# A test-time learner between transformer layers: products that share their stationary operand are made as one

## The reference

```
def recon(W1, b1, W2, b2, z):                 # W1 32x128, W2 128x32
    return z + gelu(z @ W1.T + b1) @ W2.T + b2

for x in batches:                             # 512 x 128, layer-normed
    z, y = x @ t_k.T, x @ t_v.T
    grads = gradient of mean((recon(params, z) - y)**2) in params
    params = params - 1e-3 * grads
    out = recon(params, x @ t_q.T)            # with the new params
```

## Time and profile before

| | |
|---|---|
| median of three runs | 2206.51 us (2203.84 to 2206.94) |
| the profiled execution | 2217.11 us |
| its span, first to last instruction | 2215.4 us |
| TensorE busy (PE) | 1622.4 us, 73% |
| VectorE busy (DVE) | 1256.2 us, 57% |
| ScalarE busy (ACT) | 1080.1 us, 49% |
| GpSimd busy (POOL) | 821.4 us, 37% |
| the learner's eight batches | L1209 of batch 0 starts at 595.32 us, L1248 of batch 7 at 772.22 us |

### The profile page before, as it was taken

How to read it: one execution, slowest core, us unless ns; L and a number is a source line. 1 busy time by engine, 2 the same in 40 slices (tenths; PEclk the granted TensorE clock), 3 DMA queues, 4 the chain that set the end, 5 groups by cost and what they waited for, 6 DMA issues and landing times. The chain is left out here.

```text
span 2215.4 us, 26050 instructions
## 1 busy us (share of the span) xinstructions
PE 1622.4 (73%) x8550; PEld 855.5 (39%) x8550; DVE 1256.2 (57%) x2743; ACT 1080.1 (49%) x2160; POOL 821.4 (37%) x1482
## 2 busy tenths in 40 slices
PE   2799999954499850715530159359999999979998
PEld 1133333213377640504430137213333333357776
DVE  3688888857443230054468812277787777535443
ACT  1377777745333330246650013127777776645554
POOL 3455555325433235170051775543444331012121
PEclk8699999986655555856755559659999999979999
DMA  3211111100000012000003112311111111010000
GB/s 97 72 67 66 66 66 65 42 1 1 1 1 0 1 56 76 29 8 1 0 2 115 38 39 23 54 71 46 54 59 58 57 58 54 13 40 10 6 10 15
DMA packets 85099, 85.21 MB, mean 38 GB/s; under 512 B 36071, under 2 KB 67665, under 8 KB 84837
## 3 DMA queue, kind: packets, MB, share of 16 engines
q1 hardware_dynamic: 75044, 76.43, 10.4%
q0 software_dynamic: 7680, 6.06, 1.7%
q10 hardware_dynamic: 2240, 1.05, 0.2%
HBM read 59.78 MB, written 25.17 MB: 38 GB/s over the span
## 5 line engine op out<-in xcount | busy, mean ns | idle before, releaser
L921 DVE TENSOR_REDUCE arena<-psum 128x2 f32<-128x1024 f32 x512 | 602.0, 1217 | 130.5 <-PE psum L720 125.8
L836 ACT ACTIVATE arena<-psum 128x512 f32<-128x512 f32 x1024 | 554.0, 595 | 141.4 <-PE psum L733 132.4
L733 PE MATMUL psum<-arena 99*128 99x512 bf16 x1024 | 312.6, 387 | 16.5 <-DMA arena<-arena 11.9
L720 PE MATMUL psum<-arena 72*128 72x512 bf16 x1024 | 286.9, 396 | 42.5 <-POOL arena L622 20.3
L743 PE MATMUL psum<-arena 128*32 128x512 f32 x2048 | 274.5, 608 | 3.0 <-ACT arena L836 1.9
L733 PEld LDWEIGHTS psum<-arena 99*128 99x128 bf16 x1024 | 74.8, 98 | 294.3 <-ACT arena L836 223.2
L720 PEld LDWEIGHTS psum<-arena 72*128 72x128 bf16 x1024 | 96.5, 101 | 184.8 <-DVE arena L921 28.5
L2409 ACT ACTIVATE arena<-arena 128x128 f32<-128x128 f32 x252 | 102.5, 481 | 103.2 <-POOL arena L2397 103.2
L2392 POOL TENSOR_SCALAR arena<-arena 128x4 f32<-128x4 f32 x80 | 22.5, 281 | 309.3 <-DVE arena L2386 304.8
L631 POOL TENSOR_TENSOR arena<-arena 128x16 bf16<-128x16 f32 x64 | 13.9, 218 | 316.5 <-DVE arena L921 222.2
L344 ACT ACTIVATE arena<-arena 128x128 f32<-128x128 f32 x192 | 76.7, 481 | 96.4 <-POOL arena L260 71.0
(11 more groups left out here) (440 smaller groups left out, 2723.2 us busy)
## 6 DMA issues: line engine op xcount, KB each, us to landing
arena<-L_q_parts SPq DMA_DIRECT2D x192, 96.0 KB
arena<-L_k_parts SPq DMA_DIRECT2D x192, 96.0 KB
L_q_parts<-arena SPq DMA_DIRECT2D x16, 384.0 KB, 3.3
L_k_parts<-arena SPq DMA_DIRECT2D x16, 384.0 KB, 3.3
arena<-in_L_ffn_w SPq DMA_DIRECT2D x1, 2048.0 KB
ec_result<-arena SPq DMA_DIRECT2D x1, 2048.0 KB
arena<-in_L_ffn_fc2s SPq DMA_DIRECT2D x1, 2048.0 KB, 16.5
ec_normed<-arena SPq DMA_DIRECT2D x1, 2048.0 KB
```

The source lines that it names most:

```text
L720: last = nc.tensor.matmul(bank[:, 512 * h:512 * h + 512], columns(q9[0:QK_ROWS], i, m // 2, 128 * (2 * (m % 2) + h), 128), columns(k9[0:QK ...
L733: nc.tensor.matmul(acts.bank(name), columns(k9[0:ROWS], i, g, 128 * k, 128), columns(q9[0:ROWS], i, g, 0, 512), start=True, stop=True).the ...
L836: nc.scalar.activation(prob[:, k % 2, g, :], acts.bank(name), ACT.Exp, scale=scale).then_inc(act_taken, 1)
L921: nc.vector.tensor_reduce(neg_max[:, i % 2, 2 * m:2 * m + 2], maxes.bank(("max", i, m)).rearrange("p (h t) -> p h t", h=2), axis=AX.X, op= ...
```

## The change

`y_map` is placed behind `u_map` in memory, so that one product of 64 columns with the turned tokens makes both the hidden sums and the part of `dh` that comes from the tokens; `hidden` makes it, and the four L1221 go. The accumulating group stays open until `hidden_gradient` adds the part with `m_map`; only the first tile's product has the start flag of the bank. `d_a` and `h_one` are placed beside each other per tile (65 columns), so that one product with the plain tokens makes both `nh` and the first gradient; `gradients` replaces `first_gradient` and `token_products`. The sums of one tile stand side by side in PSUM now (`a_dh`), and `nh`, `g` and `hh` are neighbours in bank 4. Waits: `y_done` moves ahead of `hidden`, `hT_done` ahead of all of `hidden_gradient`, `gradients` waits for `hh_done` and `da_done`, and ScalarE's copy of `nh` waits for the first gradient's copy on VectorE (`g_done`).

```diff
--- before.py
+++ after.py
@@ -1117,8 +1117,9 @@
     w2 = c.take(HID + 1)
     w2T = c.take(128)
     b1, b1_col = c.take(HID), c.take(1)
-    maps = c.take(2 * HID)
-    y_map, m_map = c.take(HID), c.take(HID)
+    three = c.take(3 * HID)
+    maps, uy_map, y_map = three[:, 0:2 * HID], three[:, HID:3 * HID], three[:, 2 * HID:3 * HID]
+    m_map = c.take(HID)
     q_map, u_map = maps[:, 0:HID], maps[:, HID:2 * HID]
 
     w_in, diff_done, turned, w_ready = sem("w_in"), sem("diff_done"), sem("turned"), sem("w_ready")
@@ -1168,9 +1169,10 @@
             nc.scalar.activation(y_map, c.bank(4)[:, 2 * HID:3 * HID], ACT.Copy).then_inc(maps_ready, 1)
             nc.scalar.activation(m_map[0:HID + 1, :], c.bank(4)[0:HID + 1, 3 * HID:4 * HID], ACT.Copy).then_inc(maps_ready, 1)
 
-    a, slope, d_a = c.take(128), c.take(128), c.take(128)
+    a, slope = c.take(128), c.take(128)
     a_sq, a_off, a_safe, gel, th, low, inv, phi, high, dens = (c.take(128) for _ in range(10))
-    h_one = c.take(TPB * (HID + 1)).rearrange("p (k h) -> p k h", k=TPB)
+    h_da = c.take(TPB * (2 * HID + 1)).rearrange("p (k h) -> p k h", k=TPB)
+    h_one, d_a = h_da[:, :, 0:HID + 1], h_da[:, :, HID + 1:2 * HID + 1]
     hT, hqT = c.take(S), c.take(S)
     d_sum, g_sum = c.take(HID), c.take(HID)
     nh_sum, hh_sum = c.take(HID + 1), c.take(HID + 1)
@@ -1179,7 +1181,7 @@
 
     ones_set, turned2, copied2, turned3, copied3 = sem("ones_set"), sem("turned2"), sem("copied2"), sem("turned3"), sem("copied3")
     summed2, summed3 = sem("summed2"), sem("summed3")
-    a_made, aT_made, q_made, dh_made, hh_made, nh_made = (sem(n) for n in ("a_made", "aT_made", "q_made", "dh_made", "hh_made", "nh_made"))
+    a_made, aT_made, q_made, dh_made, hh_made = (sem(n) for n in ("a_made", "aT_made", "q_made", "dh_made", "hh_made"))
     g_made, kg_made, gb_made, w2_made, o_made, y_made = (sem(n) for n in ("g_made", "kg_made", "gb_made", "w2_made", "o_made", "y_made"))
     a_done, hT_done, h_done, slope_done, hq_done = (sem(n) for n in ("a_done", "hT_done", "h_done", "slope_done", "hq_done"))
     sq_done, th_done, safe_done, gel_done, low_done, pool_step, step = (
@@ -1189,9 +1191,10 @@
 
     p_aT, p_a, p_q, p_o, p_w = (c.bank(n) for n in range(5))
     turn_bank, bias_bank = c.bank(5), c.bank(7)
-    dh, g, kg = p_a[:, 128:256], p_a[:, 256:288], p_a[:, 384:448]
+    a_dh = p_a[:, 0:256].rearrange("p (k h) -> p k h", k=TPB)
+    kg = p_a[:, 384:448]
     gb, gb_col = bias_bank[:, 0:HID], bias_bank[0:HID, HID:HID + 1]
-    nh, hh, g_w2 = p_w[:, 0:33], p_w[0:33, 64:97], p_w[:, 128:161]
+    nh_g, nh, g, hh, g_w2 = p_w[:, 0:65], p_w[:, 0:33], p_w[:, 33:65], p_w[0:33, 65:98], p_w[:, 128:161]
     y_new, m_new, w2T_new = p_w[:, 192:224], p_w[0:33, 256:288], p_w[0:33, 384:512]
 
     ROUNDS = B + 11
@@ -1205,8 +1208,10 @@
             def hidden(b):
                 pe.wait_ge(copied2, b + 1)
                 pe.wait_ge(moved, b)
+                pe.wait_ge(y_done, 3 * b)
                 for k in range(TPB):
-                    last = nc.tensor.matmul(p_a[:, 32 * k:32 * k + 32], tile_T(b, k), u_map, start=True, stop=True)
+                    last = nc.tensor.matmul(a_dh[:, k, :], tile_T(b, k), uy_map, start=(k == 0), stop=True,
+                                            skip_group_check=True)
                 last.then_inc(a_made, 1)
                 nc.tensor.matmul(p_aT[0:HID, :], u_map, c.nT[:, b, 1:S + 1], start=True, stop=True).then_inc(aT_made, 1)
 
@@ -1215,14 +1220,11 @@
                 nc.tensor.matmul(p_q[0:HID, :], q_map, c.nT[:, b, 1:S + 1], start=True, stop=True).then_inc(q_made, 1)
 
             def hidden_gradient(b):
-                pe.wait_ge(y_done, 3 * b)
                 pe.wait_ge(a_done, b + 1)
+                pe.wait_ge(hT_done, b + 1)
                 for k in range(TPB):
-                    nc.tensor.matmul(dh[:, 32 * k:32 * k + 32], tile_T(b, k), y_map, start=True, stop=False)
-                    if k == 0:
-                        pe.wait_ge(hT_done, b + 1)
-                    last = nc.tensor.matmul(dh[:, 32 * k:32 * k + 32], hT[0:HID + 1, 128 * k:128 * k + 128], m_map[0:HID + 1, :],
-                                            start=False, stop=True)
+                    last = nc.tensor.matmul(a_dh[:, k, HID:2 * HID], hT[0:HID + 1, 128 * k:128 * k + 128], m_map[0:HID + 1, :],
+                                            start=False, stop=True, skip_group_check=True)
                 last.then_inc(dh_made, 1)
 
             def hidden_products(b):
@@ -1231,17 +1233,12 @@
                     last = nc.tensor.matmul(hh, h_one[:, k, :], h_one[:, k, :], start=(k == 0), stop=(k == TPB - 1))
                 last.then_inc(hh_made, 1)
 
-            def first_gradient(b):
+            def gradients(b):
+                pe.wait_ge(hh_done, b + 1)
                 pe.wait_ge(da_done, b + 1)
                 for k in range(TPB):
-                    last = nc.tensor.matmul(g, c.n[:, TPB * b + k, :], d_a[:, 32 * k:32 * k + 32], start=(k == 0), stop=(k == TPB - 1))
+                    last = nc.tensor.matmul(nh_g, c.n[:, TPB * b + k, :], h_da[:, k, :], start=(k == 0), stop=(k == TPB - 1))
                 last.then_inc(g_made, 1)
-
-            def token_products(b):
-                pe.wait_ge(hh_done, b + 1)
-                for k in range(TPB):
-                    last = nc.tensor.matmul(nh, c.n[:, TPB * b + k, :], h_one[:, k, :], start=(k == 0), stop=(k == TPB - 1))
-                last.then_inc(nh_made, 1)
 
             def first_step(b):
                 pe.wait_ge(g_done, b + 1)
@@ -1300,8 +1297,7 @@
                 if inside(b):
                     hidden_gradient(b)
                     hidden_products(b)
-                    first_gradient(b)
-                    token_products(b)
+                    gradients(b)
                     first_step(b)
                 if inside(b - 1):
                     output(b - 1)
@@ -1351,7 +1347,8 @@
             def products(b):
                 act.wait_ge(hh_made, b + 1)
                 nc.scalar.activation(hh_sum[0:HID + 1, :], hh, ACT.Copy).then_inc(hh_done, 1)
-                act.wait_ge(nh_made, b + 1)
+                act.wait_ge(g_made, b + 1)
+                act.wait_ge(g_done, b + 1)
                 nc.scalar.activation(nh_sum, nh, ACT.Copy).then_inc(nh_done, 1)
 
             def output(b):
@@ -1430,7 +1427,7 @@
                 dve.wait_ge(a_made, b + 1)
                 if b >= 1:
                     dve.wait_ge(b_moved, 2 * b)
-                tt(by_tile(a), by_tile(p_a[:, 0:128]), b1.unsqueeze(1).to_broadcast([128, TPB, HID]), ALU.add).then_inc(a_done, 1)
+                tt(by_tile(a), a_dh[:, :, 0:HID], b1.unsqueeze(1).to_broadcast([128, TPB, HID]), ALU.add).then_inc(a_done, 1)
 
             def slopes(b):
                 dve.wait_ge(safe_done, b + 1)
@@ -1447,9 +1444,9 @@
             def hidden_gradient(b):
                 dve.wait_ge(slope_done, b + 1)
                 dve.wait_ge(dh_made, b + 1)
-                tt(d_a, dh, slope, ALU.mult).then_inc(da_done, 1)
+                tt(d_a, a_dh[:, :, HID:2 * HID], by_tile(slope), ALU.mult).then_inc(da_done, 1)
                 dve.wait_ge(da_done, b + 1)
-                nc.vector.tensor_reduce(d_sum, d_a.rearrange("p (k h) -> p h k", k=TPB), axis=AX.X, op=ALU.add).then_inc(sum_done, 1)
+                nc.vector.tensor_reduce(d_sum, d_a.rearrange("p k h -> p h k"), axis=AX.X, op=ALU.add).then_inc(sum_done, 1)
 
             def keep_gradient(b):
                 dve.wait_ge(g_made, b + 1)
```

## The result

The changed kernel takes 2191.65 us (median of 4 runs, 2188.68 to 2192.58), beside 2206.73 for the kernel before on the same chip (4 runs). The ratio is 0.992, with a 95% interval of 0.9903 to 0.9936, so it is 14 to 21 us faster. The forecast was 2194.3, or 12.2 us faster, with a range of 2186 to 2202.

What follows compares the result with a forecast made beforehand. TensorE's program order looked like the bound, with the slope chain close behind. Leg B 8.1 plus leg A 6.15 minus new waits 2.1 gave 12.2 us: 2206.5 to 2194.3, forecast 2189 to 2199, 8-in-10 range 2186 to 2202.

Steps and rivals of the forecast that it cites:

- leg B: First gradient's start to `first_step`: eight products become four, the copy of g becomes exposed; 25.73 us falls by 8.1.
- the bound of 1.8: Leg B at high clock: VectorE's reduction and norm statistics before the copy hold `first_step` at about 1.8 us.
- Leg A: `hidden`'s start to the first gradient: y products move into `hidden`, 33-row products stay; 6.15 us saved over the batches.
- The slope chain: Leg A: L1209, bias, square, GpSimd, reciprocals, L1445, then L1450; holds batches 1 to 3 at 8.1 us.
- The new wait: `hidden` waits for the y_done copies on ScalarE: 0.70 us each in batches 1 to 3, 2.1 lost.
- leg C: From `first_step` to the next `hidden`, containing the turn L1283; claimed to keep its instructions and length.
- the cover: Batches 4 and 5: the GpSimd chain hides `hidden`'s 1.85 us later start; without it, 1.85 lost in each.
- rival 2: The y_done wait passes through in batches 4 and 5, 33-row products cost their upper bound; 6.5 us saved, 2200; chance 0.13.
- 1, TensorE sets everything: TensorE's order sets legs A and B in every batch; some 30 us saved, 2176; chance 0.08.
- 3, columns in the open: Widened products' added columns aren't hidden by weight loads: 0.85 us a batch, 6.8 in all; 2201; chance 0.06.
- 4: Legs B and C held by ScalarE's norm before the turn, absorbing gain; 4 us left, 2202.5; chance 0.06.
- 5: Learner's granted clock falls to 0.50 throughout as new waits add idle time; 25 us lost, 2219; chance 0.03.

Runs made afterwards that it cites:

- e8: Changed kernel with GpSimd's residual add of the second norm moved behind both sets of factors; 2183.37 us, ratio 0.9868 to the kernel before.
- the second profile of before: The kernel before run once more without an edit, for its profile; 2209.49 us.
- e2: Kernel before with only the y products merged into `hidden`, the two gradient products left apart; 2198.65 us, ratio 0.995.
- e3: Changed kernel with the gradient products widened from 65 to 128 columns by zeros; 2190.56 us, ratio 0.9906 to the kernel before.
- e6: Changed kernel with ScalarE's norm o3 moved ahead of its copy of the turned tokens; 2187.36 us, ratio 0.9883 to the kernel before.
- e1: Kernel before with only the gradients merged as 65-column products, y products left in hidden_gradient; 2201.39 us, ratio 0.9962.
- e3 to e6: Includes two more: kernel before, y products ahead of m products instead of in pairs, ratio 0.9953; changed kernel, bias_gradient ahead of first_step, ratio 0.9895.
- a1: The changed kernel run again without an edit, on another chip; 2206.11 us, ratio 0.9911 to the kernel before.
- e9: Changed kernel with bias_gradient behind gradients, norms o3 and x3 and second_maps with its copies earlier, residual add behind factors; 2183.24 us, ratio 0.9801 to the kernel before.

## Why the prediction was right, and where it was off
The direction and the range held. The profiled learner got 13.6 us shorter (12.2 forecast) and the median 15.1. The 12.2 came so near by two errors of opposite sign, 1.9 too little in leg B and 0.45 too much in legs A and C.
- *Leg B*: 10.0 us against 8.1. Five batches took 2.22 to 2.26, as worked out (2.2), and batch 3, in part at full clock, 1.86. Batches 6 and 7 took 1.36 at nearly full clock, and the bound of 1.8 failed. VectorE has no norm statistics of x2 left to make there, so nothing stands in front of the copy:

```profile
757.16 1.08 PE L1240 MATMUL psum<-arena 128*128 128x65 f32 x8 [0.59 <-DVE arena L1447]
758.27 0.19 DVE L1453 COPY arena<-psum 128x32 f32<-128x32 f32 x1 [0.85 <-PE psum L1240]
758.38 0.86 DVE L2380 BATCH_NORM_STATS2 arena<-arena 128x6 f32<-128x128 f32 x4
...
758.52 0.64 PE L1245 MATMUL psum<-arena 128*128 128x32 f32 x2 [0.28 <-DVE arena L1453]
```

The 1.8 was too high even where statistics do stand in front of the copy. In batch 2 of e8, at full clock, the copy starts right behind them and the leg takes 1.47:

```profile
634.77 1.11 PE L1240 MATMUL psum<-arena 128*128 128x65 f32 x8 [0.28 <-ACT arena L1349]
...
636.03 0.16 DVE L1453 COPY arena<-psum 128x32 f32<-128x32 f32 x1
636.24 0.41 PE L1245 MATMUL psum<-arena 128*128 128x32 f32 x2 [0.36 <-DVE arena L1453]
```

- *Leg A*: batch 0 8.07 (7.75 forecast), 1 to 3 8.20 (8.1), 6 and 7 7.08 and 7.22 (7.3). The slope chain is the bound in batches 1, 3, 4, 5 and 7, and TensorE's products with hh's copy behind them in 0, 2 and 6. In batches 1 to 3 the two end nearly together, and that batch 2 came out at the forecast 8.1 is luck: the wait named for it was the other one. e8 shows the two apart: with the slope chain shortened leg A falls to 7.33 with a full-clock stretch and stays at 8.21 without. In the forecast for batches 6 and 7 the terms add up to 6.9 at the lower end, not 7.05.
- *The new wait*: 0.82 in batches 1 to 3 with the slightly longer products, 0.70 forecast. In batches 4 and 5 leg C grew by 1.95 and the gradients stayed 12.1 and 13.15 us from the turn (11.98 and 13.08 before): the cover held, and rival 2 did not come. Legs A and C together: 3.6 us saved, 4.05 forecast.
- *What the sum lacked* is the clock. I took leg A of before from one profile, in which seven batches had a full-clock stretch, and counted no gain in batch 2. In the second profile batch 2 took 10.50. What the change is worth in leg A there depends on the stretch: 0 with it, 2.3 without it. That is consistent with the 15.9 us between the learners of the second profile of before and the changed kernel, and with a median gain above the sum; how often each batch of before lacks the stretch was not measured.
- *Rivals*: 1, TensorE sets everything, falls by e2. 3, columns in the open, falls by e3: the rule of the Trainium skill behind it ("TensorE: Matmul & The Clock Gate", Part 3, overlap only across row groups) does not hold for these products, where 63 more columns cost 0.09 us in four instead of 0.84. 4 fell with leg B's gain arriving whole. 5: the changed kernel did have fewer full-clock stretches (five instead of seven), and leg A lost nothing by it, since in batches 2 and 4 it is as long without one. In batch 6 or 7 a missing one would have cost 1.0 (e6, e8).

## What to carry to other kernels
Merging products with the same stationary operand paid here because a product with 128 weight columns took nearly the same time with 32, 64, 65 or 128 moving columns; but look at what the removed product covered (here a copy) and what the merged one must wait for earlier (here an operand copied just before). Where two chains end within 1 us, cut the loop into legs and ask for each leg which chain ends last, at either clock. A kernel whose bound alternates with TensorE's clock shows its gain in one profile only in part: take the legs from two.

## What the runs showed of the hardware
- Four 32-bit products of 128 weight columns are followed by the next shape after 1.85 us with 32 moving columns, after 1.87 with 64, at clock 0.50; 128 columns instead of 65 add 0.09 to 0.11 to four.
- Alternating between operands of 128 and of 33 rows costs 0.8 us in eight products at clock 0.50 (4.51 against 3.69), 0.14 for each change.
- GpSimd's residual add stretches a simultaneous VectorE instruction with two inputs in SBUF from 0.29 to between 1.24 and 1.28 us (batches 1 to 4 of the changed kernel); apart from each other it takes 0.29 again (e8). The Trainium skill ("GPSIMD Engine Reference", Key points) has GpSimd share its SBUF interfaces with VectorE, with contention for instructions of two SBUF inputs, and the runs agree.
- The section with expert choice and rotary attention, which no edit touches, took 785.1 to 785.2 us (e1, e2, e8), 788.2 to 788.7 (the second profile of before, the changed kernel, e3 to e6), 798.7 (the first profile of before) or 802.4 to 802.5 (a1 and e9, both on the last chip). Why is open.
